# A factorisation tower on one core: the first layer's 105 f32 products become three f32r products each, with the parts split on ScalarE and GpSimd

## The reference

```python
x0 = xk = e                                   # [512, 39, 16]
for W in (f0, f1, f2):                        # f0 [39*39, 128], f1, f2 [128*39, 128]
    z = einsum('bfd,bgd->bfgd', x0, xk).reshape(b, f * g, d)
    xk = einsum('bpd,pm->bmd', z, W)          # 128 maps
    outs.append(xk)
z = concatenate(outs, axis=1).sum(-1)         # [512, 384]
h = relu(concatenate([z, dense_ctx], 1) @ W_top1 + b_top1)
y = relu(h @ W_top2 + b_top2) @ W_top3
```

## Time and profile before

| | |
|---|---|
| three runs | 805.65, 807.54 and 807.4 us, median 807.4 |
| the profiled execution | 809.94 us, span 808.1 |
| TensorE matmul | 698.5 us, 86% of the span |
| VectorE | 621.5 us, 77% |
| ScalarE | 488.2 us, 60% |
| GpSimd | 256.1 us, 32% |
| mean granted TensorE clock | 0.979 |

### The profile page before, as it was taken

One profiled execution on the slowest core, in us unless ns is written; L12 is line 12 of the kernel. 1 busy time (PEld: TensorE's weight loads), 2 busy tenths in 40 slices (PEclk: granted clock), 3 DMA queues, 4 the chain that ended last, 5 costly groups with the idle time before them and its releaser, 6 DMA issues.

```text
span 808.1 us, 12253 instructions
## 1 busy us (share of the span) xinstructions
PE 698.5 (86%) x3327; PEld 498.2 (62%) x3327; DVE 621.5 (77%) x1409; ACT 488.2 (60%) x1659; POOL 256.1 (32%) x247
## 2 busy tenths in 40 slices
PE   0107899999999999999999979999999998999977
PEld 0002556666667776666666766666666686767757
DVE  1004698999999885799899865799899986799960
ACT  0002566776778663776677644676678564768851
POOL 6750026432661240812741330622651000211110
PEclk9999799999999999999999999999999999999989
DMA  3710202120212020020302020020202010020000
GB/s 82 282 41 1 72 10 61 25 70 13 66 22 72 10 64 22 5 80 2 85 4 80 2 66 21 4 75 8 77 12 72 9 57 25 3 78 1 2 0 1
DMA packets 23423, 33.96 MB, mean 42 GB/s; under 512 B 7816, under 2 KB 10616, under 8 KB 22967
## 3 DMA queue, kind: packets, MB, share of 16 engines
q1 hardware_dynamic: 18230, 31.84, 12.8%
q0 software_dynamic: 5120, 1.29, 1.9%
HBM read 9.13 MB, written 0.00 MB: 11 GB/s over the span
## 4 chain that ended last, share of the span: by engine, by line
PE 49%; DVE 25%; issue 11%; another core or an unknown queue 8%; ACT 5%; DVEq 1%; DMA 0%; SPq 0%; ACTq 0%
DVE sums L621 12%; PE x_ps L738 10%; PE v_ps L713 5%; PE v_ps L715 5%; PE v_ps L714 5%; PE s_ps L766 4%; PE a_ps L713 4%; PE a_ps L714 4%; PE a_ps L715 4%; DVE z_sb L594 3%; ACT scaled L419 3%; DVE scaled L564 2%; DVE sums L569 2%; PE s_ps L845 2%
## 5 line engine op out<-in xcount | busy, mean ns | idle before, releaser
L419 ACT ACTIVATE scaled<-a_ps,x0c 128x128 f32<-128x128 f32 x1216 | 352.2, 385 | 211.1 <-PE a_ps L715 187.6
L621 DVE SCALAR_TENSOR_TENSOR sums<-v_ps,x0c,sums 128x128 f32<-128x128 f32 x768 | 215.4, 341 | 59.2 <-PE v_ps L715 54.6
L363 POOL DMA_INDIRECT e_sb<-in_tables,ids_now x140 | 166.5, 1189 | 40.3 <-issue 38.1
L713 PE MATMUL v_ps<-w_hi,x_hi 128*128 128x512 f32 x320 | 175.8, 549 | 4.0 <-DVE w_lo L537 2.0
L379 POOL TENSOR_TENSOR diag_sb<-x0c,eye_sb 128x320 f32<-128x320 f32 x64 | 63.2, 988 | 360.3 <-PE s_ps L845 357.2
L738 PE MATMUL x_ps<-z_sb,w_sb 117*128 117x512 f32 (+1 forms) x210 | 115.0, 629 | 20.4 <-DVE z_sb L594 18.8
L715 PE MATMUL v_ps<-w_hi,x_lo 128*128 128x512 f32 x320 | 127.6, 399 | 0.0
L714 PE MATMUL v_ps<-w_lo,x_hi 128*128 128x512 f32 x320 | 127.5, 399 | 0.0
L713 PE MATMUL a_ps<-w_hi,x_hi 128*128 128x512 f32 (+1 forms) x320 | 124.4, 389 | 0.6 <-issue 0.5
L714 PE MATMUL a_ps<-w_lo,x_hi 128*128 128x512 f32 (+1 forms) x320 | 123.5, 386 | 0.0
L715 PE MATMUL a_ps<-w_hi,x_lo 128*128 128x512 f32 (+1 forms) x320 | 123.2, 385 | 0.0
(11 more groups left out here) (77 smaller groups left out, 659.4 us busy)
## 6 DMA issues: line engine op xcount, KB each, us to landing
b_sb<-a_sb SPq DMA_DIRECT2D x300, 78.0 KB
w_sb<-in_w SPq DMA_DIRECT2D x1, 2496.0 KB
e_sb<-in_tables,ids_now POOLq DMA_INDIRECT x140
s_sb<-in_w SPq DMA_DIRECT2D x2, 1024.0 KB
wt_sb<-in_wt SPq DMA_DIRECT2D x1, 768.0 KB
s_sb<-in_w SPq DMA_DIRECT2D x1, 512.0 KB
wt_sb<-in_wt SPq DMA_DIRECT2D x1, 512.0 KB
w_raw<-in_w0a SPq DMA_DIRECT2D x1, 409.5 KB
```

The lines of the kernel that those rows point to most:

```text
L363: pool.indirect_dma_start(out=e_sb[0:rows, i, :], out_offset=None, in_=tables, in_offset=bass.IndirectOffsetOnAxis(ap=ids_now[0:rows, 0, i ...
L419: last = nc.scalar.activation(scaled[:, s % 2, to, j, :], bank[:, j * MAPS:(j + 1) * MAPS], ACT.Copy, scale=x0c[:, k % 4, s, lo + j:lo + j ...
L621: nc.vector.scalar_tensor_tensor(out=sums[:, s % 2, j, :], in0=v_ps[n % 2][:, j * MAPS:(j + 1) * MAPS], scalar=x0c[:, k % 4, s, lo + j:lo ...
L713: nc.tensor.matmul(to, high, w_high, start=True, stop=False)
```

## The change

The parts of w0 are made once: w0_hi by ScalarE before the second round of w1, w0_lo by VectorE, queued behind the second pair's first split. For each of the 105 products, VectorE's z0_sb is as before, ScalarE rounds it to z0_hi (f32r) in the same step, ahead of its scalings, GpSimd subtracts to get z0_lo (f32r), also in the same step, and TensorE two steps after z0, behind its a group, adds three f32r matmuls into x1_ps. VectorE's z0_sb now waits for z0_lo of two before. GpSimd puts diag_sb into its queue one step earlier than TensorE uses it, ahead of z0_lo. The steps Z0_AT and S_AT move. z_first gives up its own memory for that of `scaled`. The first chunk's seven products stay in f32.

```diff
-Z0_AT = (2, 4, 7, 9, 12, 14, 15)
-X1_AT = tuple(h + 1 for h in Z0_AT)
+Z0_AT = (2, 4, 6, 8, 10, 12, 14)
+X1_AT = tuple(h + 2 for h in Z0_AT)
...
-S_AT = ((1, 4, 6, 9), (10, 12, 14, 17), (2, 6, 11, 17), (2, 6, 11, 17))
+S_AT = ((1, 5, 7, 9), (11, 13, 15, 17), (3, 7, 11, 17), (3, 7, 11, 17))
...
+        w0_hi = sb("w0_hi", [3 * F0, T0, MAPS], f32r)
+        w0_lo = sb("w0_lo", [3 * F0, T0, MAPS], f32r)
...
-        z_first = sb("z_first", [3 * F0, T0, COLS])
+        z0_hi = sb("z0_hi", [3 * F0, 2, COLS], f32r)
+        z0_lo = sb("z0_lo", [3 * F0, 2, COLS], f32r)
...
+        z_first = scaled.rearrange("p a g f m -> p (a g f m)")[0:3 * F0, 0:T0 * COLS]\
+            .rearrange("p (i c) -> p i c", c=COLS)
...
# GpSimd
-                    if h in diag_at and exists(t, k - 1):
-                        s = diag_at.index(h)
+                    if h + 1 in diag_at and exists(t, k - 1):
+                        s = diag_at.index(h + 1)
...
+                    if h in Z0_AT and k >= 0 and exists(t, k + 1):
+                        q = Z0_AT.index(h)
+                        rows, n0 = T0_ROWS[q], T0 * (4 * t + k) + q
+
+                        pool.wait_ge(z0_hi_ready, n0 + 1)
+                        nc.gpsimd.tensor_tensor(z0_lo[0:rows, q % 2, :], z0_sb[0:rows, q % 2, :],
+                                                z0_hi[0:rows, q % 2, :].bitcast(fp32),
+                                                ALU.subtract).then_inc(z0_lo_ready, 1)
# ScalarE
+                    if h in Z0_AT and k != -1 and exists(t, k + 1):
+                        q = Z0_AT.index(h)
+                        rows, n0 = T0_ROWS[q], T0 * (4 * t + k) + q
+                        act.wait_ge(z0_ready, n0 + T0 + 1)
+                        if not isinstance(t, int) or n0 >= 2:
+
+                            act.wait_ge(x1_step, n0 + T0 - 1)
+                        nc.scalar.activation(z0_hi[0:rows, q % 2, :], z0_sb[0:rows, q % 2, :],
+                                             ACT.Copy).then_inc(z0_hi_ready, 1)
...
+                act.wait_ge(w0_ready, 1)
+                nc.scalar.activation(w0_hi[:, :, :], w0_sb[:, :, :], ACT.Copy).then_inc(w0_hi_ready, 1)
                 round_w1(1)
# VectorE
-                        dve.wait_ge(x1_step, n0 - 1)
+                        if not isinstance(t, int) or T0 * (4 * t + k) + q >= 2:
+                            dve.wait_ge(z0_lo_ready, n0 - T0 - 1)
...
                 split_first(1)
+                dve.wait_ge(w0_hi_ready, 1)
+                nc.vector.tensor_tensor(w0_lo[:, :, :], w0_sb[:, :, :], w0_hi[:, :, :].bitcast(fp32),
+                                        ALU.subtract).then_inc(w0_lo_ready, 1)
# TensorE, ahead of the v group
-                        pe.wait_ge(z0_ready, T0 * 4 * t + T0 * (k + 1) + q + 1)
...
-                        nc.tensor.matmul(x1_ps[:, :], w0_sb[0:rows, q, :], z0_sb[0:rows, q % 2, :],
-                                         start=(q == 0), stop=(q == T0 - 1)).then_inc(x1_step, 1)
# TensorE, behind the a group
+                        pe.wait_ge(z0_lo_ready, T0 * 4 * t + T0 * k + q + 1)
...
+                        high = z0_hi[0:rows, q % 2, :]
+                        nc.tensor.matmul(x1_ps[:, :], w0_hi[0:rows, q, :], high, start=(q == 0), stop=False)
+                        nc.tensor.matmul(x1_ps[:, :], w0_hi[0:rows, q, :], z0_lo[0:rows, q % 2, :],
+                                         start=False, stop=False)
+                        nc.tensor.matmul(x1_ps[:, :], w0_lo[0:rows, q, :], high,
+                                         start=False, stop=(q == T0 - 1)).then_inc(x1_step, 1)
```

More of the change, by code:

```diff
@@ L211, in dlrm_tower @@
         z0_ready = sem("z0_ready")
+        z0_hi_ready = sem("z0_hi_ready")
+        z0_lo_ready = sem("z0_lo_ready")
+        w0_hi_ready = sem("w0_hi_ready")
+        w0_lo_ready = sem("w0_lo_ready")
         x1_step = sem("x1_step")
@@ L730, in slot @@
                         turn_first(1)
-                    if h in X1_AT and k != -1 and exists(t, k + 1):
-                        q = X1_AT.index(h)
-                        rows = T0_ROWS[q]
-                        pe.wait_ge(z0_ready, T0 * 4 * t + T0 * (k + 1) + q + 1)
-                        if q == 0:
-                            pe.wait_ge(sum0_done, 4 * t + k + 1)
-                        nc.tensor.matmul(x1_ps[:, :], w0_sb[0:rows, q, :], z0_sb[0:rows, q % 2, :],
-                                         start=(q == 0), stop=(q == T0 - 1)).then_inc(x1_step, 1)
                     if h == XC_AT and exists(t, k + 1):
@@ L824, in slot @@
                         group(a_ps[n % 2], t, k, s, A_FIELDS[i]).then_inc(a_group_done, 1)
+                    if h in X1_AT and k != -1 and exists(t, k + 1):
+                        q = X1_AT.index(h)
+                        rows = T0_ROWS[q]
+                        if isinstance(t, int) and t == 0 and k == 0 and q == 0:
+                            pe.wait_ge(w0_lo_ready, 1)
+                        pe.wait_ge(z0_lo_ready, T0 * 4 * t + T0 * k + q + 1)
+                        if q == 0:
+                            pe.wait_ge(sum0_done, 4 * t + k + 1)
+                        high = z0_hi[0:rows, q % 2, :]
[4 more added lines that the diff above has]
+                                         start=False, stop=(q == T0 - 1)).then_inc(x1_step, 1)
                     if turns_x0:
```

## The result

| | median of the runs | ratio to before |
|---|---|---|
| before | 806.9 us (4 runs, 805.65 to 807.54) | |
| changed | 833.1 us (4 runs, 831.49 to 833.48) | 1.0323 [1.0303, 1.0342] |

The forecast was 808.3 us in a range of 797 to 820. The change costs 26 us. The profiled executions, 809.94 us before and 833.48 after, differ by 23.5 us in span (808.1 to 831.6), at the same mean granted clock of 0.979.

What follows compares the result with a forecast made beforehand. VectorE was taken to bound the chunks without MLP, TensorE the MLP pairs. The terms -5.6 - 6 + 11 + 1 + 1.5 - 1 gave +0.9 us on the median 807.4: 808.3 us, range 797 to 820.

Steps and rivals of the forecast that it cites:

- shorter product, TensorE-bound chunks: 42 products in six MLP chunks, each 0.16 to 0.26 us shorter: -8.5 us, of which 3.0 is not collected.
- wait for z0 there: TensorE's wait for z0 in the six MLP chunks goes: 7.5 us at most, 2.5 taken.
- VectorE's idle time, chunk 0 with it: Eight chunks without MLP recover 6 of 15.6 us of VectorE idle time; chunk 0 gains about 1.
- ScalarE's roundings: Seven roundings a chunk, 4.2 us on ScalarE, with nothing on the path: zero, with 0.3 us of cover.
- collisions: z0_lo's SBUF reads stretch VectorE's two-tile sums: +11 us in eight chunks, +2.4 in the MLP chunks.
- queue: GpSimd's queue of gathers, z0_lo and diag runs late in odd chunks: 5.6 us or nothing, +1 taken.
- start: Making w0_hi and w0_lo delays VectorE's second split, for which TensorE waits: +1.5 us, once in a run.
- the price of a z0_lo to VectorE, 0.2 us by place: Each z0_lo costs VectorE 0.2 us, bounds 0.05 and 0.4, since multiply-adds cover it at four steps.
- The length: A z0_lo on GpSimd takes 1.05 us, upper end 1.16, scaled by elements from diag_sb.
- Rival 3: GpSimd's queue is the new bound: odd chunks +5 to 6, gathers late for e_parts, 814 us; chance 0.11.
- sum of 22.2 us against 20: Odd chunks, z0_lo of step 4 to 14: 10 gathers, 5 z0_lo, 2 diag against ten steps' time.
- rival 2: Decoupling wins: z0_lo lies under multiply-adds (-8), TensorE's waits in MLP pairs go (-3), 797.5 us; chance 0.28.

Runs made afterwards that it cites:

- e12: The changed kernel without GpSimd's z0_lo; the second of the three matmuls takes z0_hi again, roundings kept: 785.86 us, 0.9755.
- e1: The changed kernel's step numbers and placement, but each product one f32 matmul again, with no high or low parts: 797.68 us, 0.9856 of before.
- e9: e1 with one wait: GpSimd issues the second pair's gathers only after TensorE has turned the first chunk's embeddings: 780.89 us, 0.9691.
- e10: As e9, with the gathers of the first pair's second chunk behind the same wait too: 782.21 us, 0.9704.
- e4: The changed kernel with one of twenty gathers per pair of chunks, z0_lo whole: 778.56 us, 0.9624.
- e8_steps_ahead: The kernel before with only the new step numbers, f32 product two steps after z0 but still ahead of the v group: 801.06 us, 0.9899.
- e11: e1 with one of twenty gathers per pair of chunks, so f32 products and no GpSimd part: 746.16 us, 0.9259.
- e5: The kernel before with one of twenty gathers per pair of chunks: 769.1 us, 0.953.

## Why the prediction was wrong

The forecast's terms, against what the experiments give for them. "Without the pause" throughout:

| term | predicted | measured | from |
|---|---|---|---|
| shorter product, TensorE-bound chunks (-8.5 + 3.0) | -5.5 | -4.3 | e12 less e1, MLP (-2.3 and -3.1 against e9, e10) |
| wait for z0 there | -2.5 | -12.4 | e1 less before, MLP |
| VectorE's idle time, chunk 0 with it (-6 - 1) | -7 | -7.7 | e1 less before, rest |
| ScalarE's roundings | 0 | +0.8 | e12 less e1, rest |
| collisions (+11 + 2.4) and queue (+1) | +14.4 | +52.0 | after less e12 |
| the pause | none | -4.3 | before and after |
| start | +1.5 | -0.5 | first v_ps matmul |
| sum | +0.9 | +23.5 | spans (the rows are rounded) |

**What held.** The bounds were read rightly: VectorE in the chunks without MLP, TensorE in the pairs. The product's 0.39 us in records, z0's wait gone (1.1 us left), the recovered VectorE idle time, ScalarE at nothing, and the gathers in time for e_parts (1.4 us of waiting) all came; the gain from the shorter product came too, at 2.3 to 4.3 us. So did the maximum of z0_lo, 2.29 us for 2.3.

**The step that failed: the price of a z0_lo to VectorE, 0.2 us by place.** It measured 0.43 to 0.60 in chunks 1 to 3, 6, 7, 10 and 11, above the upper bound of 0.4, and 59.3 / 105 = 0.56 us of VectorE busy time each (680.9 less e12's 621.6). Two parts of the argument were wrong. The length: 1.05, at most 1.16, was scaled from diag_sb, which reads one tile and a broadcast column. GpSimd's row:

```profile
L399 POOL TENSOR_TENSOR z_lo<-z_sb,z_hi x105: 1257/1297/2294, 93.5 to 758.4; 117x512 fp32r<-117x512 f32 x90, 78x512 fp32r<-78x512 f32 x15
```

The shortest is 1.257, the mean 1.51. It no longer fits under four multiply-adds (a row of 1.11), so even the well-placed one reaches into the sum behind them. The place: the prediction compared only the two lengths. In chunk 7, z0 ends at 405.81 and z0_lo starts 0.82 us later, close to the 0.7 foreseen. But the four multiply-adds that "cover it" began 0.3 us before it, at 406.33, and the next sum starts at 407.37: a z0_lo of 1.05 us would have reached 0.3 us into that sum as well, and the real one reaches 0.54. Of the 15 z0_lo of each step, those that hold up a VectorE operation number 14, 5, 5 and 15 at steps 2, 6, 8 and 12, which the prediction took as covered, and 6, 8 and 11 at steps 4, 10 and 14, where it saw no cover; with few gathers (e4) it is 14, 7, 5 and 15, and 6, 8 and 12. At steps 4 and 14 it is z0_lo that stands, behind the 1024 sum, with a mean of 1.92 and 2.00 us. The right length alone would not have saved it: from 0.165 per diag_sb, shortest by shortest, it gives 0.165 x 1.257/0.72 = 0.29, for 68 operations 20 us.

The Trainium skill (SBUF — State Buffer, "SBUF: two separate sides") says that the one that starts first holds the port pair for its whole instruction and the other fully blocks. The trace agrees: the z_sb at 417.20 ended 2.40 us later, behind two whole operations, and 79 of the 91 stretched operations end as if they had stood until GpSimd was done. The prediction set this aside because the mean per diag was small. The mean per operation, 0.56 of 1.5 us, is how often and how far they overlap, and not a softer rule.

**The second: GpSimd's queue at +1.** Rival 3 had the right place (odd chunks at its pace) and was given 0.11; it cost 17.7 us and not 5 to 6. Its sum of 22.2 us against 20 was made with z0_lo at 1.05 and diag_sb at 1.0 for two of them. With the measured 10 x (1.21 + 0.30) + 5 x 1.51 + 2 x 1.06 it is 24.8 against 20. And it asked only whether z0_lo would be late for its matmul, which has two steps; the wait came at "Diag moves a step earlier in the queue and s_ps a step later, at no cost while the queue keeps up". diag_sb has one step, stands behind the gathers and the z0_lo of the step before, and s_ps is ahead of the v group on TensorE. "Against: GpSimd is busy only 32%" read an average where a stretch counts: in the odd chunks it was 92.0 of 158.0 us before, the gaps between gathers not counted, and the change took it to 134.5 of 183.6.

**A size that was off the other way.** The wait for z0 in the MLP chunks was worth 12.4, not 2.5, and e8_steps_ahead gives 11.6 of that for distance alone; with few gathers, where there is next to no pause, e11 less e5 gives 12.5. The prediction had bounded it at 7.5 from the wait row and cut it to 2.5 by TensorE's idle time; but an f32 product that waits ahead of the v group delays that group and everything the others do with it, which no single wait row sums. How the 12.4 divides among these was not measured.

**The start.** w0_hi and w0_lo did not wait for 81. The changed kernel's rows of ScalarE and VectorE:

```profile
77.41 0.60 ACT L487 ACTIVATE a_sb<-pair_ps 117x512 f32<-117x512 f32 x1 [0.52 <-PE pair_ps L782]
...
77.91 0.94 ACT L525 ACTIVATE w_hi<-w_sb 117x896 fp32r<-117x896 f32 x1
...
78.88 1.09 DVE L679 TENSOR_TENSOR w_lo<-w_sb,w_hi 117x896 fp32r<-117x896 f32 x1 [3.38 <-ACT w_hi L525]
...
81.09 1.28 DVE L566 TENSOR_TENSOR w_lo<-v_ps,w_hi 128x512 fp32r<-128x512 f32 x2
```

w0_hi came at 77.91, its record starting 0.1 us ahead of a_sb's end. From a_sb to the second split it is 3.68 us where it was 2.67, so the term was 1.0 and not 1.5. But a_sb itself came 1.5 us earlier than before, and the first chunk began 0.5 earlier. Why a_sb came earlier is not shown.

Without GpSimd's part the kernel takes 785.9 us, better than rival 2's 797.5: the gains were larger than reckoned, mostly by the placement, and the cost larger still. The errors partly cancel (gains of 24 us where 15 were forecast, a cost of 52 for 14), and the pause shrank by 4.3 for no known reason: the price of GpSimd's part was further off than the result shows.

The chain that ended last names this, too. By line, shares of the span:

```profile
POOL e_sb L373 11%; POOL z_lo L399 6%; DVE sums L651 5%; POOL diag_sb L389 4%; PE s_ps L790 3%; ACT scaled L437 2%; PE v_ps L746 1%; PE v_ps L748 1%; PE v_ps L747 1%; DVE z_sb L624 1%; DVE scaled L583 1%; PE a_ps L748 1%; PE a_ps L746 1%; PE a_ps L747 1%; DMA e_sb<-in_tables,ids_now 1%
```

GpSimd's gathers, z0_lo and diag_sb make 21% of a chain in which an engine at 51% busy would have seemed free.

## What to carry to other kernels

An elementwise operation handed to GpSimd is no help to a VectorE that works on SBUF tiles: here 105 subtractions of 117x512 cost it as much busy time beside it (59 us) as on it (58), and sizes of the work already there, scaled by length, gave too little (20 us for 31 to 34). Work out when it starts, how long a row of the same form takes, and whether it ends before VectorE's next operation with two SBUF inputs; that it is shorter than what runs beside it is not enough. Ask of a queue that gets longer which of those in it has the least slack; here that was diag_sb with one step, not the new work with two. And try a change's placement apart from its arithmetic: without the pause, distance and place were worth 20 us with the old f32 product (24 between e5 and e11), the f32r split without its low part 3.5. In the medians, pause and all, they are 9 and 12.

## What the runs showed of the hardware

- While indirect transfers are issued at the start, TensorE's tiny matmuls come singly, 0.5 to 2.6 us apart in steps of about 0.7; without them 64 take 0.69 us. The gathers cost the kernel before 25.3 us ahead of the first chunk (87.3 to 62.0) and 16.1 in the chunks, 10.3 without the pause. The reason is open.
- A subtraction of 117x512 with an f32r output takes GpSimd 1.26 us at least and up to 2.29 beside VectorE; ScalarE's rounding of the same tile takes 0.64.
- VectorE's operations with two SBUF inputs that meet such a subtraction or a diag_sb end a full length less 0.12 us after it (79 of 91); those that read PSUM and one SBUF tile keep their means of 339 to 344 ns.
- TensorE and VectorE stand idle together, for 4.4 and 4.2 us in the longest case, at one place of the loop's body and not in the unrolled copy, and TensorE's clock is at its lower level behind it. It costs up to 6.8 us a pass and 0.1 to 11.9 us in all, nothing in some passes. Its cause is open.
